# A megakernel of two transformer layers: the gated recurrence begun earlier among ternary quantisation, its update kept in PSUM, its thresholds applied by groups of 64 columns

## What is computed

```python
# GLA, per batch, 16 heads, key width 8, value width 16
S = S * exp(g_t)[..., None] + k_t[..., None] * v_t[..., None, :]
o_t = einsum('bhk,bhkd->bhd', q_t, S)
o = silu(g) * groupnorm(o);  x = x + o @ Wo;  x = x + (silu(n @ W1) * (n @ W3)) @ W2
# ternary feed-forward, on the same normed input
scale = clip(mean(abs(w_g)), 1e-8)                 # groups of 64 weights, bf16
w_hat = clip(round(w_g / scale), -1, 1) * scale;   w = w + (w_hat - w)
h = silu(x @ w_gate.T) * (x @ w_up.T);  y = rms_norm(h) @ w_proj.T
```

## Time and profile before

| | us |
|---|---|
| median of 3 runs | 757.46 (755.2 to 760.0) |
| profiled execution | 756.01 |
| its span, first to last instruction | 754.2 |
| TensorE busy in it | 585.8 (78%) |
| VectorE busy | 539.3 (72%) |
| ScalarE busy | 319.8 (42%) |
| GpSimd busy | 263.1 (35%) |

### The profile page before, as it was taken

The page is one execution under the profiler, slowest core; times in us unless marked ns, Lnnn a source line. Parts: engine busy times, 40 slices in busy tenths (PEclk is TensorE's granted clock), DMA queues, the critical chain, the costliest instruction groups (busy, mean ns, idle before and its releaser), DMA issues.

```text
span 754.2 us, 11132 instructions
## 1 busy us (share of the span) xinstructions
PE 585.8 (78%) x3698; PEld 418.1 (55%) x3698; DVE 539.3 (72%) x1129; ACT 319.8 (42%) x581; POOL 263.1 (35%) x242
## 2 busy tenths in 40 slices
PE   3933567977665878999577998898887869999990
PEld 2721345645442666888434565455454458888880
DVE  5868997978779665776396876886886157777753
ACT  2376533323110212345304664454454546666640
POOL 3147476835456653427565001001004401211210
PEclk9975669989777889999757999999998999999996
DMA  5101200000011200075999563442001696000005
GB/s 185 54 31 56 80 2 0 1 1 0 0 29 53 58 27 1 1 178 127 177 264 125 69 79 57 68 58 31 2 2 58 233 421 256 27 24 29 30 22 181
DMA packets 43623, 58.39 MB, mean 77 GB/s; under 512 B 7184, under 2 KB 37072, under 8 KB 42544
## 3 DMA queue, kind: packets, MB, share of 16 engines
q1 hardware_dynamic: 41696, 52.55, 29.6%
q0 software_dynamic: 1872, 5.13, 1.9%
HBM read 41.97 MB, written 15.51 MB: 76 GB/s over the span
## 4 chain that ended last, share of the span: by engine, by line
PE 36%; DVE 11%; DMA 3%; issue 2%; ACT 2%; POOL 1%; SPq 0%; ACTq 0%; POOLq 0%; DVEq 0%
PE bank L750 17%; DVE small L1701 5%; PE bank L997 4%; PE bank L974 4%; PE bank L947 4%; PE bank L744 4%; DMA pieces<-P 2%; PE bank L949 1%; PE bank L976 1%; DMA yt<-results 1%; POOL P L2135 1%; DVE mtok L1712 1%; PE bank L1014 1%; ACT PTa L1273 1%; DVE XA L1730 0%
## 5 line engine op out<-in xcount | busy, mean ns | idle before, releaser
L1701 DVE TENSOR_REDUCE small<-bank 128x1 f32<-128x256 f32 (+3 forms) x256 | 107.3, 482 | 10.4 <-PE bank L949 9.5
L2040 POOL TENSOR_TENSOR al<-hm,ah 128x512 fp32r<-128x512 f32 (+1 forms) x28 | 40.9, 1462 | 92.8 <-ACT ah L1236 89.8
L947 PE MATMUL bank<-Ks,Qs 96*128 96x256 bf16 (+3 forms) x256 | 67.2, 330 | 5.3 <-DVE small L1701 3.7
L1979 DVE TENSOR_TENSOR wl<-wall,wh 128x1024 fp32r<-128x1024 f32 x46 | 56.1, 1221 | 19.8 <-ACT wh L1387 19.8
L974 PE MATMUL bank<-Qs,Ks 99*128 99x512 bf16 (+3 forms) x256 | 59.1, 308 | 4.9 <-issue 4.5
L1273 ACT ACTIVATE PTa<-bank 128x512 f32<-128x512 f32 (+1 forms) x96 | 43.6, 528 | 29.9 <-PE bank L976 29.6
L1273 ACT ACTIVATE PTb<-bank 128x512 f32<-128x512 f32 (+1 forms) x96 | 43.7, 529 | 28.2 <-PE bank L976 27.8
L949 PE MATMUL bank<-maskb,identb 128*128 128x128 bf16 x256 | 55.6, 236 | 0.0
L1572 DVE TENSOR_TENSOR_SCAN S<-AT,U 128x512 f32<-128x512 f32 x32 | 49.2, 1537 | 8.8 <-POOL QS L2058 8.5
L974 PEld LDWEIGHTS bank<-Qs,Ks 99*128 99x128 bf16 x256 | 25.4, 99 | 46.9 <-issue 29.9
L750 PE MATMUL bank<-XTh,wgu 128*128 128x512 f32 x64 | 35.6, 556 | 20.2 <-DVE hm L1526 20.2
(11 more groups left out here) (351 smaller groups left out, 1640.7 us busy)
## 6 DMA issues: line engine op xcount, KB each, us to landing
wall<-e_pack SPq DMA_DIRECT2D x8, 1536.0 KB, 12.1
pieces<-P SPq DMA_DIRECT2D x12, 512.0 KB, 10.1
Qs<-pieces SPq DMA_DIRECT2D x48, 128.0 KB, 5.4
Ks<-pieces SPq DMA_DIRECT2D x48, 128.0 KB, 6.1
stg<-w_pack SPq DMA_DIRECT2D x18, 256.0 KB, 2.7
wf<-t_pack SPq DMA_DIRECT2D x12, 256.0 KB, 2.7
sorted_rows<-blank SPq DMA_DIRECT2D x1, 2944.0 KB, 13.1
yt<-results SPq DMA_DIRECT2D x8, 256.0 KB, 4.2
```

Of the source, the lines that this page charges most:

```text
L947: nc.tensor.matmul(banks[b][:, o:o + w], Q[0:96, h, i * P:(i + 1) * P], K[0:96, h, 0:w], start=True, stop=False)
L1701: last = nc.vector.tensor_reduce(mxv[:, i, h:h + 1], banks[b][:, o:o + w], AX.X, ALU.max, negate=True)
L1979: nc.vector.tensor_tensor(flat(moe["wl"][:, i % 2, half]), wall[:, bass.ds(place + half * KC * EI, KC * EI)], flat(moe["wh"][:, i % 2, hal ...
L2040: nc.gpsimd.tensor_tensor(al[0:M, s % 3, :], hm[0:M, s % 3, :], ah[0:M, s % 3, :].bitcast(F32), ALU.subtract).then_inc(*alr.tick(s))
```

## The change

`T_AHEAD` becomes 1: one piece is quantised ahead of the recurrence and the other eleven in turns 0 to 10 (before, eight in turns 0 to 7). `z`, `e1` and `sp` of batch 1 move into turns 0, 1 and 3, so that the recurrence begins once the decay of batch 0 is made. The feed-forward steps go to turns 5 + int(1.6 s), and the gate's `silug` from turns 2 to 5 to turns 6 to 9. GpSimd finishes three pieces in place of six.

The update is written over the replicated values in their PSUM bank, and the scan reads it there. The tile U goes, and `rep` i waits for scan i - 2 in place of update i - 2.

The comparison and the multiplication become one `tensor_scalar` with two operations for each group of 64 columns, eight for a piece, with half the scale and the scale read per partition. The scale is made in bf16, copied to f32, and halved from the bf16 value.

```diff
-        ff_slot = {4 + int(1.5 * s): s for s in FF}
+        ff_slot = {5 + int(1.6 * s): s for s in FF}
...
-            return i < 6
+            return i < 3
...
-        T_AHEAD = 4
+        T_AHEAD = 1
         ORDER = [("norm", 0, 0), ("norm", 0, 1), ("tr", 0), ("norm", 1, 0), ("norm", 1, 1), ("cast",), ("proj", 0), ("tr", 1),
-                 ("z", 0)] + early(0) + [("e1", 0), ("proj", 1), ("sp", 0)] + early(1)
-        ORDER += [("z", 1)] + early(2) + [("e1", 1)]
-        for q_ in range(3, T_AHEAD):
-            ORDER += early(q_)
-        later[0] = [("sp", 1)]
+                 ("z", 0)] + early(0) + [("e1", 0), ("proj", 1), ("sp", 0)]
+        later[0], later[1], later[3] = [("z", 1)], [("e1", 1)], [("sp", 1)]
         for c in range(NC):
             for pr in range(2):
-                later[2 + 2 * c + pr] = [("silug", c, pr)]
+                later[6 + 2 * c + pr] = [("silug", c, pr)]
...
-                claim(d % 2, ug, i)
+                claim(d % 2, sc, i)
...
-                scl, half, thr = small[:, 5, 0:G // 2].bitcast(BF16), small[:, 7, 0:G // 2].bitcast(BF16), small[:, 6, 0:G]
+                scl, thr = small[:, 5, 0:G // 2].bitcast(BF16), small[:, 6, 0:G]
+                step, half = small[:, 7, 0:G], small[:, 7, G:2 * G]
...
-                link(nc.vector.tensor_scalar(half, thr, 1.0 / 128, 0.5e-8, ALU.mult, ALU.max))
+                tell(nc.vector.tensor_copy(step, scl))
+                link(nc.vector.tensor_scalar(half, scl, 0.5, None, ALU.mult))
...
-                link(nc.vector.tensor_tensor(g3(ms), g3(ab), spread(half), ALU.is_gt))
+                for g in range(G):
+                    gs = slice(g * 64, (g + 1) * 64)
+                    ins = nc.vector.tensor_scalar(ms[:, gs], ab[:, gs], half[:, g:g + 1], step[:, g:g + 1], ALU.is_gt, ALU.mult)
...
-                if i >= 3:
-                    dve.wait_ge(*sc.upto(i - 3))
-                nc.vector.tensor_tensor(L0["U"][:, i % 3, :], L0["KT"][:, c * CH:(c + 1) * CH], banks[i % 2][:], ALU.mult)\
+                nc.vector.tensor_tensor(banks[i % 2][:], L0["KT"][:, c * CH:(c + 1) * CH], banks[i % 2][:], ALU.mult)\
                     .then_inc(*ug.tick(i))
...
-                nc.vector.tensor_tensor_scan(L0["S"][:, i % 2, :], L0["AT"][:, c * CH:(c + 1) * CH], L0["U"][:, i % 3, :], 0.0,
+                nc.vector.tensor_tensor_scan(L0["S"][:, i % 2, :], L0["AT"][:, c * CH:(c + 1) * CH], banks[i % 2][:], 0.0,
                                              ALU.mult, ALU.add).then_inc(*sc.tick(i))
```

More of the change, by code:

```diff
@@ L177, in plan @@
             return made, o
[L180 removed]
+        r0, o = plan([("VTh", [2, NC * CH], F32R), ("VTl", [2, NC * CH], F32R),
                       ("S", [2, CH], F32), ("QS", [2, CH], F32)], region)
@@ L1494, in quantize @@
                 i = PIECES.index(p)
-                scl, half, thr = small[:, 5, 0:G // 2].bitcast(BF16), small[:, 7, 0:G // 2].bitcast(BF16), small[:, 6, 0:G]
+                scl, thr = small[:, 5, 0:G // 2].bitcast(BF16), small[:, 6, 0:G]
+                step, half = small[:, 7, 0:G], small[:, 7, G:2 * G]
                 ab, ms = L0["ab"][:, i % 2, :], L0["ms"][:, i % 2, :]
-                g3 = lambda t: t.rearrange("p (g n) -> p g n", n=64)
-                spread = lambda t: t.unsqueeze(2).broadcast_to([P, G, 64])
                 dve.wait_ge(*t_abs.upto((p, 0)))
-                link(nc.vector.tensor_reduce(thr, g3(ab), AX.X, ALU.add))
-                tell(nc.vector.tensor_scalar(scl, thr, 1.0 / 64, 1e-8, ALU.mult, ALU.max))
-                link(nc.vector.tensor_scalar(half, thr, 1.0 / 128, 0.5e-8, ALU.mult, ALU.max))
+                link(nc.vector.tensor_reduce(thr, ab.rearrange("p (g n) -> p g n", n=64), AX.X, ALU.add))
+                link(nc.vector.tensor_scalar(scl, thr, 1.0 / 64, 1e-8, ALU.mult, ALU.max))
+                tell(nc.vector.tensor_copy(step, scl))
+                link(nc.vector.tensor_scalar(half, scl, 0.5, None, ALU.mult))
                 if i >= 2:
                     dve.wait_ge(*t_sgn.upto(PIECES[i - 2]))
-                link(nc.vector.tensor_tensor(g3(ms), g3(ab), spread(half), ALU.is_gt))
+                for g in range(G):
+                    gs = slice(g * 64, (g + 1) * 64)
+                    ins = nc.vector.tensor_scalar(ms[:, gs], ab[:, gs], half[:, g:g + 1], step[:, g:g + 1], ALU.is_gt, ALU.mult)
+                    if g < G - 1:
+                        tell(ins)
                 if pool_finishes(i):
-                    nc.vector.tensor_tensor(g3(ms), g3(ms), spread(scl), ALU.mult).then_inc(*t_done.tick(p))
+                    ins.then_inc(*t_done.tick(p))
                 else:
-                    link(nc.vector.tensor_tensor(g3(ms), g3(ms), spread(scl), ALU.mult))
+                    link(ins)
                     link(nc.vector.tensor_tensor(ms, ms, ab, ALU.subtract))
```

## The result

The changed kernel takes 776.72 us (median of 4 runs, 774.96 to 779.42), the kernel before 757.55 beside it on the same chip (755.2 to 760.0). The ratio is 1.025, interval 1.022 to 1.028. I had said 747, with 735 to 761 as the range: the sign was wrong too. The profiled execution is the one of 774.96, with a span of 773.2 us.

A forecast was written before the change was run, and what follows sets the result against it. VectorE was taken to bound the first stretch, VectorE and TensorE by turns the second. 756.0 less 5 and 5 made 746; with the runs' median 1.4 above the profiled execution, 747 us, range 735 to 761.

The forecast's parts named there:

- rep's wait on the scan: 0, bound +4: Second stretch: replication waiting for scan i - 2 stays hidden and costs 0 us, at most +4.
- With the new spacing there is none in either turn: -5.: Second stretch: turns 20 and 26 hold no feed-forward step ahead of batch 0's output copies; -5 us, bounds -10 replaced by -8 and 0.
- half of the 10 us passes through, -5: Second stretch: scans reading PSUM lose GpSimd's 10 us of lock, half reaching the total; -5 us, bounds -10 and 0.
- C: Rival: TensorE's queue sets the second stretch and the block of eight costs 2.3 us, so no gain; 757 us, chance 0.18.
- First stretch, -5: From 44.3 us until feed-forward step 4 is issued: end at 117.3 us against 122.26, -5 us.
- the 6 us that I had set aside for such holds: First stretch: allowance of 6 us for VectorE operations held by GpSimd.
- B: Rival: the eight short operations run at the pace of small ones, 0.8 us per block; 735 us, chance 0.17.
- The early start: First stretch: starting the recurrence sooner only fills VectorE's idle time and removes no work; scan 0 near 54 to 58 us.
- Tail, +3 and +4: End of second stretch: last feed-forward steps three turns later, +3 us; weight splits beside small operations of `rms`, +4 us.
- D: Rival: replication waiting on the scan starves TensorE and lowers the granted clock, deciding from about 0.7; 762 us, chance 0.12.
- E: Rival: scan or update out of a PSUM bank pay 0.2 us more each; 760 us, chance 0.03.

The follow-up runs named there:

- wait_alone: Kernel before, with only replication i waiting for scan i - 2 in place of update i - 2, update still in SBUF: 768.2 us, ratio 1.0137.
- psum_alone: Kernel before, with the update written over its PSUM bank, the scan reading it there, and replication waiting for the scan: 756.56 us, ratio 1.0000.
- psum_order_15: Changed kernel with the old broadcast quantisation and feed-forward steps in their old turns, 4 + int(1.5 s), replication first: 756.03 us, ratio 0.9989.
- after_broadcast: Changed kernel with comparison and multiplication as broadcast 128x512 operations again; new order and update in PSUM kept: 782.01 us, ratio 1.0193, on a slower chip.
- psum_late: Kernel before with the update in PSUM and replication behind the feed-forward matmuls that begin in its turn: 756.81 us, ratio 0.9877, on a slower chip.
- groups_alone: Kernel before with only the quantisation changed to eight two-scalar operations of 64 columns and the copied scale: 762.54 us, ratio 1.0076.
- after_late: Whole change, with replication moved behind the feed-forward matmuls that begin in its turn: 753.61 us, ratio 0.9952 to the kernel before.
- psum_order_late: Changed kernel with the old broadcast quantisation and replication behind the feed-forward matmuls that begin in its turn: 759.14 us, ratio 0.9885, on a slower chip.
- order_alone: Kernel before with only the new order: early start, feed-forward steps at 5 + int(1.6 s), GpSimd finishing three pieces: 755.27 us, ratio 0.9972.
- psum_order_15_late: Changed kernel with old broadcast quantisation, old feed-forward turns, and replication behind the feed-forward matmuls that begin in its turn: 742.4 us, ratio 0.9820.
- psum_spacing: Kernel before with the update in PSUM, replication first, and feed-forward steps moved to 5 + int(1.6 s): 770.09 us, ratio 1.0186.

## Why the prediction was wrong

Ratios in a row give the budget (in per cent of 757.5 us): the claim +1.37 (wait_alone); free scans -1.37 (psum_alone less wait_alone); early start -0.1 (psum_order_15 less psum_alone); spacing +2.0 (after_broadcast less psum_order_15); groups +0.6 (the change less after_broadcast). Together +2.5, the 19 us measured. Each step carries 0.3 to 0.5% of uncertainty, so that the early start isn't told from nothing, and each holds for the kernel on which it was measured: what the spacing costs depends on the claim.

**The step that failed: "rep's wait on the scan: 0, bound +4".** I wrote that replication is hidden, since the next to need it is the update, and that `in` waited for `hm` behind that scan in any case. The second was true in part (the 20.2 us of waits for hidden tiles are gone), but the waits for scans are four times that. Both sentences look at who needs replication; neither at what is queued behind it when the scan itself is late. A scan is late whenever VectorE's last item of a turn waits for TensorE, and the timeline above shows the circle. The runs showed +10.4 us with the old order (wait_alone), outside the bound. With the new spacing, moving replication gives back 3.0% of the whole change (1.025 to 0.995), 23 us. The forecast even named the queue behind the wait, and then did not walk a turn of the output path with it.

**"With the new spacing there is none in either turn: -5."** Turns 20 and 26 are indeed free of a step, but a copy reads the matmuls of a projection at the end of TensorE's turn, and in 21, 27 and 29 these now stand behind a step, and the whole turn behind the scan. In turns 20 and 26 the waits did shrink, from 3.34 and 4.74 to 2.31 and 2.48; but in turns 21 and 27, where before no such wait stood, `otok` waits 5.91 (182.46 in the timeline above) and `X1l` 6.58. Right place, wrong sign: I checked two turns, not every one in which the path has an item.

**Free scans, "half of the 10 us passes through, -5".** The mechanism was right: 1.216 us each, never held, update at 0.674. The term was mis-sized. With the claim in place 10.4 us came through, more than the scans' own 7.4. Without the claim it can't be had, since the scan needs the bank, so no run shows the term by itself against the kernel before. C's objection (TensorE sets the second stretch) falls by this gain and by psum_late, which has the same matmuls and is 1.2% under the kernel before. The Trainium skill (SBUF — State Buffer, Who interferes with whom) states that a VectorE instruction with two SBUF inputs contends with GpSimd's reads and one with at most one doesn't, outside certain fast modes. The runs agree: 1.642 us on average for the one, 1.216 for the other.

**First stretch, -5; measured +7.7.** The error is 12.7 us, and by my own terms the small operations come to as much: 11 blocks took 32.6 us in place of 20.4, +12.2; 11 casts 7.2 in place of 11 undisturbed ones of 0.17, +5.3; 11 scales 2.6 for 1.9, +0.8; less the 6 us that I had set aside for such holds: 12.3. Much of that is no net loss, for GpSimd gets in somewhere in a piece in any case. In after_broadcast the two operations that the block replaces take 22.4 us in all and the subtractions and additions behind them 17.8; in the change the blocks take 32.6, the casts 7.2 and those behind only 7.6. That is 7.2 us more, and scan 9 moves by 7.1 us (122.9 to 130.0). The block's undisturbed price was good (1.74 for 1.85; B with 0.8 falls), but few blocks are undisturbed. Timeline of the changed kernel, VectorE's casts and blocks, then GpSimd beside the last of them:

```profile
67.06 1.74 DVE L1505 TENSOR_SCALAR ms<-ab,small 128x64 bf16<-128x64 bf16 x8
...
87.06 1.27 DVE L1499 CAST small<-small 128x8 f32<-128x8 bf16 x1
...
88.44 3.86 DVE L1505 TENSOR_SCALAR ms<-ab,small 128x64 bf16<-128x64 bf16 x8
...
87.01 1.30 POOL L2039 TENSOR_TENSOR al<-hm,ah 128x512 fp32r<-128x512 f32 x1 [4.17 <-ACT ah L1233]
...
88.85 1.15 POOL L2032 TENSOR_TENSOR wq<-ms,sgn 128x512 bf16<-128x512 bf16 x1
89.96 1.26 POOL L2057 TENSOR_TENSOR QS<-QT,S 128x512 f32<-128x512 f32 x1
```

A block stands at 1.74 with GpSimd idle and at 3.86 here. `wq` begins at 88.85 between two of the eight, and `QS` follows at 89.96. Each that slips in costs VectorE about 1 us. Eight short operations leave seven gaps between them, and up to three were used. I gave this as what would make the forecast too low and put no price on it. Over the whole kernel the groups cost 0.6 to 0.8% (groups_alone 0.76; after_late less psum_order_late 0.67), some 5 us. The same rule of the Trainium skill lets a tensor-scalar operation or a cast take the shared port for one instruction; that it is given up again between two of them is what this block shows.

**The early start.** Scan 0 begins at 56.53, within the 54 to 58 forecast and 13.7 us before. As forecast, starting sooner removed little: order_alone gives 0.3%, and the early start 0.1% with replication first; with replication late it is worth 0.6%, give or take 0.5 (psum_order_15_late less psum_late, from two chips). The lead is eaten by pieces: in order_alone scan 0 begins 15.3 us earlier and scan 8 only 7.6 (114.7 for 122.3).

**Tail, +3 and +4.** The weight splits end at 266.29, within the 3 us of SwiGLU's start that I gave, and small operations of `rms` are held, but only five of them (0.43 to 1.27 us, between 254.0 and 258.8): the 13 from 253.2 to 259.2 average 0.42, not over 0.6. The term looks somewhat too large; it wasn't tested apart. Nor was the +3 for the later feed-forward steps, which the spacing's cost (see psum_spacing) may well contain.

**The rivals.** D came nearest, place and sign right: replication on the scan starves TensorE. Its price was taken by way of the clock, which went from 0.86 to 0.82 over the second stretch, far above the 0.7 from which I had it decide. The idle time costs directly. The range left out that both stretches could go wrong at once: the first stretch's 12.7 us alone would make 760 of 747, inside it, the second's 17.2 (138.2 for 121.0) alone 764, just outside; together they make the 777 that was measured. B's 0.8 us per block, C (no gain) and E (a dear PSUM operand) all fall: 1.74 undisturbed, psum_late 1.2% under the kernel before, 1.216 and 0.674.

## What to carry to other kernels

Before a wait is added, put down where in an in-order queue it stands and walk one whole turn in which the producer is itself late: if it can wait for something queued behind the new wait, the two engines alternate. The same wait, placed behind work that doesn't need it, turned 1.019 into 0.989 here. Where two engines lock each other out, a long operation split into eight can be held several times, here up to three; price it with the neighbour busy, not from a quiet row.

## What the runs showed of the hardware

- A scan with one operand in a PSUM bank takes 1.216 us on average over 32, the longest 1.221, and was never held by GpSimd; with both in SBUF 1.22 undisturbed and 1.64 on average.
- GpSimd gets in between VectorE operations that follow each other without a wait: the same eight operations took 1.74 with it idle, 2.70 with one of its operations in between, 3.86 with two and the end of a third, 4.5 with three.
- A cast of 8 columns per partition can take 1.27 us beside a GpSimd operation, 0.17 without (the cast at 87.06 above; its median neighbour 0.17).
- Two-scalar operations of 64 bf16 columns follow each other every 0.21 us (1.74 for eight, the last of which takes 0.295): 0.03 for the columns by an estimate from the earlier trace rows, the rest fixed. The Trainium skill (VectorE: DVE Perf Modes, on the trn2 errata) gives 58 cycles plus the columns over the mode's speed, an estimated 0.08, and says itself that this comes out too low for a single operation; the measurement decides against the 0.08.
